# Layer norm of the rows behind attention: the scale and shift applied on ScalarE instead of VectorE

## The chip, the cores and the metric

The kernel runs on one core of a Trainium2 chip. The metric is the device time of one launch in microseconds (us). The names used below are those of the core's engines: TensorE (PE; its weight loads are PEld), VectorE (DVE), ScalarE (ACT), GpSimd (POOL) and SyncE (SP), each with its own queue of instructions that it works through in order.

## The reference

One transformer layer over 8 batches of 512 tokens of width 256: causal attention with 16 heads, a layer norm on the sum, a mixture of experts (16 experts, 6 for each token, and a shared one), and a second layer norm.

```
def _layernorm(x, axis=-1, eps=1e-05):
    m = jnp.mean(x, axis=axis, keepdims=True)
    v = jnp.var(x, axis=axis, keepdims=True)
    return (x - m) / jnp.sqrt(v + eps)
...
    x = L0_attn_x
    x = _layernorm(x + _L0_attn_ref(x, L0_attn_w_qkv, L0_attn_w_out), axis=-1)
    x = _layernorm(x + _L0_ffn_ref(x, ...), axis=-1)
    return x
```

The change touches the first of these two layer norms, for the rows of seven of the eight batches.

## The kernel before

**Stages.** The first part of the kernel (up to about 480 us of its span) is attention, batch by batch. Behind it come the shared expert (with the rest of the last batch in between), the blocks of routed experts, and the final sum with the second layer norm.

**The order inside a batch.** A batch `b` is four groups of four heads, `g` = 0 to 3, and each group has eight sub-steps `s` = 0 to 7. Each engine runs its own unrolled loop over `(g, s)`, and tables written by hand say what it does at which sub-step. On PE the string `PE_ORDER[g][s]` is the order of its work in a sub-step:

- `P`: `scores` (line 873), the key-by-query scores of this group that the softmax needs. There are twelve fills of a PSUM bank, numbered 0 to 11, and they take turns in two banks: fill n waits until ScalarE has done the exponential of fill n - 2 (`pe.wait_ge(exp_done, ...)`). Sub-step 0 has fills 0 and 1, sub-step 1 has 2 and 3, sub-step 2 has 4 and 5, sub-step 3 has 6 and 7, and 4 to 7 have one each. Fills 4 to 7 are 384 columns wide.
- `F` and `G`: `scores_for_max` (lines 854 and 860), scores of the group after the next, whose row maxima VectorE takes (`maxima`, line 1629); eleven fills in three banks, so that each waits for the maximum three before it.
- `A`: `attend` (line 885), probabilities times values of the group before, or the transposes of its result (line 911).
- `M`: one stage of the work in between, by the table `MISC`: projections for the next batch, the transpose of the maxima (`m`), and for the batch before it the output projection (`p0`, `p1`), the transposes of the normalised rows (`x0`, `x1`, line 917) and the router (`r`, `d`).

**ScalarE** (`iteration` under `@block.scalar`) does at each sub-step the first `PROBS_AHEAD[g][s]` of the exponentials (`probabilities`, line 1243), then what `MISC` gives it, then the rest of the exponentials. In group 2 this is: sub-step 1: exponentials 2 and 3, then two small copies for stage `m` (`shift_h` and `shift`, line 1234); sub-step 2: exponential 4, then 5; sub-step 3: 6 and 7, then `attn_T`; sub-step 4: 8, then the copies `t_hi` and `t_raw` of stage `x0`.

**VectorE** does at each sub-step its share of the maxima and a list of other work. The layer norm of batch `b - 1` runs in iteration `b`: the sum with the input into `x1p` at (1,4) and (1,6), the statistics `stats` and `mean_var` at (1,5) and (1,6); GpSimd makes `rstd` from them at (1,7) (`inverse_std`, lines 2127 and 2130); VectorE normalises two of the four row tiles of 128x256 at (2,1) and the other two at (2,2) (`normalize`, line 1645). The tables for group 2:

```
PE_ORDER[2] = ["FAPMG", "PFAMG", "FPMGA", "PAMFG", "FAMPG", "FPGAM", "AFPMG", "FPGAM"]
PROBS_AHEAD[2] = [1, 2, 1, 2, 1, 2, 1, 2]
MAXIMA_AHEAD[2] = [1, 2, 2, 1, 1, 2, 0, 2]
```

Stage `x0` stands at (2,4), ahead of `P` there; PE waits in it for both halves of the rows (`pe.wait_ge(x1_done, 2 * b)`). SyncE waits for the same count before it loads the next `x_res`. In the last of the seven iterations there are no maxima to take, and PE runs filler matmuls in their place (line 981). The rows of the eighth batch are normalised in the epilogue, by the old function on VectorE, which the change leaves there.

Of the kernel before, what the change touches and what calls it, by code (L numbers as in the profile page):

```python
# [24 lines left out]
P = 128  # L25
B, S, D = 8, 512, 256
# [3 lines left out]
QT = S // P  # L30
# [77 lines left out]
STATS_AT = {(1, 5): 0, (1, 6): 1}  # L108
INVERSE_AT = (1, 7)
NORMALIZE_AT = {(2, 1): 0, (2, 2): 1}  # L110
ROUTE_AT = {(3, 1): 0, (3, 2): 1, (3, 4): 2, (3, 5): 3, (3, 6): 4}
SOFTMAX_AT = (3, 2)

# [85 lines left out]
CLEARED, CONSTS = 11, 14  # L199
Y_PIECES = B - 1  # L200
Y_ROWS = P * -(-(T_ALL + P) // (P * Y_PIECES))
GAP, GAP2 = 352, 3672


def fills_of(g, s):

    done = sum(FILLS_OF_SUB[g][:s])
    return tuple(range(done, done + FILLS_OF_SUB[g][s]))
# [44 lines left out]
def postln_layer(nc, xT, x, wqk, wv, wo, gw, gb, ws, we, be, b13, b2s, out):  # L253
    fp32, f32r, bf16 = mybir.dt.float32, mybir.dt.float32r, mybir.dt.bfloat16
    i32, u32 = mybir.dt.int32, mybir.dt.uint32
    ALU, ACT, AX = mybir.AluOpType, mybir.ActivationFunctionType, mybir.AxisListType
# [5 lines left out]
    def sem(name):  # L262
        return ctx.enter_context(nc.semaphore(name))

    def sb(name, shape, dt=fp32, where=ctx):
        return where.enter_context(nc.sbuf_tensor(name, shape, dt))

    def sa(name, shape, dt=fp32):
        return sb(name, shape, dt, phase_a)

    with ctx:
# [12 lines left out]
        mean_var = sb("mean_var", [P, QT, 2])  # L284
        var_eps = sb("var_eps", [P, QT])
        rstd = sb("rstd", [P, QT])
        bias = sb("bias13", [P, 2, ST])
# [72 lines left out]
        expert_of = sa("expert_of", [P, 2])  # L360
        skipped_rows = sa("skipped_rows", [P, 2])
        table_rows = sa("table_rows", [4, P], i32)
        bias_rest = sa("bias_rest", [P, GAP2])
        x1p = [sa(f"x1p{n}", [P, QT, PAY]) for n in range(2)]
        index = [sa(f"index{n}", [P, QT * TOP_K], u32) for n in range(2)]
# [99 lines left out]
        t_lo_done = sem("t_lo_done")  # L465
        ln_step = sem("ln_step")
        rstd_step = sem("rstd_step")
        x1_done = sem("x1_done")
        x1_stored = sem("x1_stored")
        router_step = sem("router_step")  # L470
# [761 lines left out]
        def _(act):  # L1232
            def copy(dst, src, scale=1.0):
                return nc.scalar.activation(dst, src, ACT.Copy, scale=scale)  # L1234

            def probabilities(G, fills):
                for f in fills:
                    kt, heads = PROB_FILLS[f]
                    n, width = len(heads), S - kt * P
                    act.wait_ge(st_full, SF * G + (f + 1))  # L1240
                    if not (isinstance(G, int) and G == 0):
                        act.wait_ge(pv_done, 4 * G + (kt - 3))
                    nc.scalar.activation(probs[kt][:, heads[0]:heads[0] + n, :],  # L1243
                                         st[f % ST_BANKS][:, 0:n * width].rearrange("p (h t) -> p h t", h=n),
                                         ACT.Exp).then_inc(exp_done, 1)
# [21 lines left out]
            def transposed(misc, k):  # L1267

                copy(t_hi[:, k, :], misc)
                return copy(t_raw[:, k, :], misc)  # L1270

            def misc_stage(b, g, stage, no, misc=None):
# [34 lines left out]
                elif stage[0] == "x":  # L1307
                    k = int(stage[1])
                    act.wait_ge(t_lo_done, 4 * t + (k + 1))
                    transposed(misc, k).then_inc(misc_free[bank], 1)  # L1310

            def middle_part(nb, tile):
                act.wait_ge(rest_done, 4 * nb + (tile + 1))
                copy(parts[tile % 2][1][:, tile // 2, :], rest[:, tile % 2, :]).then_inc(part_m_done, 1)

            def read_attn(G):
                act.wait_ge(pv_done, 4 * G + 4)
                if not (isinstance(G, int) and G == 0):
                    act.wait_ge(recip_done, G)
                copy(attn_T[:], ov).then_inc(attn_T_done, 1)  # L1320
# [13 lines left out]
            def iteration(b, par):  # L1334
                whole = isinstance(b, int)
                for g in range(NG):
                    G = 4 * b + g
                    for s in range(SUBS):
                        probabilities(G, PROB_FILLS_OF_SUB[s][:PROBS_AHEAD[g][s]])
                        if s == READ_AT and not (whole and b == 0 and g == 0):  # L1340
                            read_attn(G - 1)
                        stage = MISC.get((g, s))
                        if stage and has(b, g, stage):
                            misc_stage(b, 1 - par if stage[0] == "v" else g, stage, fill_no(b, (g, s)))
                        if (g, s) in PARTS_AT and not (whole and b == LAST):
                            middle_part(b + 1, PARTS_AT[g, s])
                        if (g, s) == SOFTMAX_AT and not (whole and b == 0):
                            router_softmax(b - 1)
                        if (g, s) == SPLIT_X_AT and not (whole and b == LAST):
                            split_x(b + 2)  # L1350
                        if whole and b == LAST and (g, s) in FIRST_W_AT:
                            split_w(FIRST_W_AT[g, s])
                        if whole and b == LAST and (g, s) == SPLIT_FIRST_X1_AT:
                            split_x1(0)
                        probabilities(G, PROB_FILLS_OF_SUB[s][PROBS_AHEAD[g][s]:])
# [248 lines left out]
        def _(dve):  # L1604
# [38 lines left out]
            def normalize(buf, done, tiles=range(QT)):  # L1643
                for qt in tiles:
                    last = nc.vector.tensor_scalar(buf[:, qt, 0:D], buf[:, qt, 0:D], mean_var[:, qt, 0:1],
                                                   rstd[:, qt:qt + 1], ALU.subtract, ALU.mult)
                last.then_inc(done, 1)
# [173 lines left out]
            def iteration(b, par):  # L1821
                whole = isinstance(b, int)
                for g in range(NG):
                    G = 4 * b + g
                    for s in range(SUBS):
                        shifts = has(b, g, "m") and (g, s) in SHIFT_AT
                        first_group = whole and b == 0 and g == 0
                        maxima_fills = () if whole and 4 * b + g + 2 >= NG * B else fills_of(g, s)
                        if shifts:
                            split_shift(G + 1, (g + 1) % 2, fill_no(b, key_of("m", g)), 2 * SHIFT_AT[g, s])  # L1830
                        if s == NORM_AT and not first_group:
                            norm_rows(G - 1, (g - 1) % NG)
                        for f in maxima_fills[:MAXIMA_AHEAD[g][s]]:
                            maxima(G + 2, (g + 2) % NG, f, g % 2)
                        if shifts and SHIFT_AT[g, s] == 0:
                            split_shift(G + 1, (g + 1) % 2, fill_no(b, key_of("m", g)), 1)
                        if s == RECIP_AT and not first_group:
                            rows_recip(G - 1)
                        if (g, s) == RANK_AT and not (whole and b < 2):
                            rank(b - 2, par, fill_no(b - 1, key_of("d")))  # L1840
                        if not (whole and b == 0):
                            if (g, s) in SUM_AT:
                                stage = f"p{SUM_AT[g, s]}"
                                misc_stage(b, 1 - par, stage, fill_no(b, key_of(stage)))
                            if (g, s) in STATS_AT:
                                f = STATS_AT[g, s]
                                attn_stats(b, 1 - par, f, fill_no(b, key_of(f"p{f}")))
                            if (g, s) in NORMALIZE_AT:
                                f = NORMALIZE_AT[g, s]
                                dve.wait_ge(rstd_step, 2 * b)  # L1850
                                normalize(x1p[1 - par], x1_done, (2 * f, 2 * f + 1))
                            if (g, s) in ROUTE_AT:
                                route(b - 1, 1 - par, fill_no(b, key_of("r")), ROUTE_AT[g, s])
                        if whole and b == LAST and (g, s) in FIRST_W_AT:
                            split_w(FIRST_W_AT[g, s])
                        if whole and b == LAST and (g, s) == SPLIT_FIRST_X1_AT:
                            low_x1(0)
                        for f in maxima_fills[MAXIMA_AHEAD[g][s]:]:
                            maxima(G + 2, (g + 2) % NG, f, g % 2)
                        if (g, s) in REST_AT and not (whole and b == LAST):  # L1860
                            tile = REST_AT[g, s]
                            rest_of(b + 1, tile, fill_no(b, key_of(QK[tile])))
                        if (g, s) == LOW_X_AT and not (whole and b == LAST):
                            low_x_of(b + 2)
# [508 lines left out]
```

## Time and profile before

| | us |
|---|---|
| median of 3 runs (lowest, highest) | 1070.45 (1070.27, 1071.28) |
| the profiled execution | 1073.4 |
| its span (first to last instruction) | 1071.6 |
| PE busy | 993.2 (93%) |
| DVE busy | 811.9 (76%) |
| ACT busy | 734.7 (69%) |
| POOL busy | 752.0 (70%) |

The profile has a page with busy shares, and the trace behind it is asked for views: the chain of waits that ended last, a timeline of an engine in a window, the busy time of all engines in a window, the instructions of one source line. Times are microseconds from the start of the span. In a timeline a row is start, length, engine, line, operation, written tile and read tiles, and a count; a length over several instructions goes from the start of the first to the end of the last, and in square brackets stands the time that the engine had been idle and what ended it. A matmul's end is modelled, and neighbouring matmuls overlap.

### The profile page before, as it was taken

What the parts mean: (1) busy time and instruction counts of PE and PEld (TensorE: products, weight loads), DVE (VectorE), ACT (ScalarE), POOL (GpSimd) and SP (SyncE); (2) the same over time, 40 slices, a digit from 0 to 9 for tenths busy, and PEclk for the clock granted to TensorE, in tenths of its full rate; (3) what the DMA queues carried; (4) which work ended last, traced back from release to release, by engine and by line L of the source; (5) the groups of instructions that cost most, each with busy time, mean ns of one, the idle gap of its engine ahead of it and who ended that gap; (6) DMA issues with size and microseconds to landing.
All of it is one profiled execution on the core that took longest, in us unless ns stands there. A gap on an engine that the chain in (4) does not pass through costs nothing.

```text
span 1071.6 us, 27815 instructions
## 1 busy us (share of the span) xinstructions
PE 993.2 (93%) x7534; PEld 791.1 (74%) x7535; DVE 811.9 (76%) x2622; ACT 734.7 (69%) x1859; POOL 752.0 (70%) x677
## 2 busy tenths in 40 slices
PE   7899999999999998899899999999999999999982
PEld 4545555656565554459889999999999999999871
DVE  8776878888888888848767687777777777777496
ACT  4577566676666665667455598878888888888545
POOL 4224548888888888877754677777777777777576
PEclk8899999999999999999899999999999999999986
DMA  6633244555555555367778988878877878788793
GB/s 183 174 113 101 85 139 153 180 163 172 161 174 171 168 167 188 124 209 222 251 227 199 214 153 159 135 129 133 131 131 130 134 130 134 131 136 175 191 385 130
DMA packets 136716, 176.37 MB, mean 165 GB/s; under 512 B 19584, under 2 KB 113840, under 8 KB 136368
## 3 DMA queue, kind: packets, MB, share of 16 engines
q1 hardware_dynamic: 88016, 105.83, 33.4%
q0 software_dynamic: 39024, 54.29, 28.7%
q10 hardware_dynamic: 9584, 15.11, 4.7%
q8 instruction: 48, 0.79, 0.3%
q14 instruction: 44, 0.36, 0.1%
HBM read 73.68 MB, written 78.17 MB: 142 GB/s over the span
## 4 chain that ended last, share of the span: by engine, by line
PE 71%; DVE 16%; ACT 5%; issue 4%; DMA 1%; POOL 1%; SPq 1%; ACTq 0%; POOLq 0%; DVEq 0%
PE psum L1118 19%; PE psum L840 11%; PE psum L1145 7%; PE psum L885 5%; PE psum L1148 4%; PE psum L873 4%; DVE rowmax L1629 4%; PE psum L854 4%; PE psum L1101 4%; PE psum L1131 2%; ACT probs L1243 2%; PE psum L1132 2%; PE psum L1082 2%; PE psum L860 1%; PE psum L917 1%
## 5 line engine op out<-in xcount | busy, mean ns | idle before, releaser
L1243 ACT ACTIVATE probs<-psum 128x512 f32<-128x512 f32 (+2 forms) x384 | 186.5, 530 | 118.8 <-PE psum L873 116.7
L1629 DVE TENSOR_REDUCE rowmax<-psum 128x1 f32<-128x512 f32 (+3 forms) x352 | 212.1, 633 | 54.3 <-PE psum L860 52.0
L2188 POOL DMA_INDIRECT xs_d<-x1p,index x192 | 204.1, 1063 | 54.3 <-issue 39.4
L1118 PE MATMUL psum<-we_hi_lo,xb_hi 128*128 x828 | 206.7, 332 | 0.0
L1976 DVE TENSOR_TENSOR hb<-psum,hb 128x176 f32<-128x176 f32 x207 | 70.7, 342 | 96.7 <-ACT hb L1424 90.8
L2260 POOL DMA_INDIRECT x_d<-y_sb,tokens x69 | 108.5, 1572 | 49.5 <-issue 28.6
L2100 POOL TENSOR_SCALAR_AFFINE_SELECT probs<-probs 128x512 f32<-128x512 f32 x128 | 87.3, 682 | 78.6 <-ACT probs L1243 76.3
L1118 PEld LDWEIGHTS psum<-we_hi_lo,xb_hi 128*128 128x128 f32 x828 | 136.9, 188 | 2.9 <-issue 0.2
L854 PE MATMUL psum<-stack_k,stack_q 96*128 96x256 bf16 (+3 forms) x512 | 129.1, 310 | 7.6 <-DMA stack_k<-k_l 2.4
L2260 POOL DMA_INDIRECT z_d<-y_sb,tokens x69 | 108.6, 1573 | 38.2 <-issue 25.3
L1118 PE MATMUL psum<-we_hi_lo,xb_lo 128*128 x414 | 133.6, 323 | 0.0
L2260 POOL DMA_INDIRECT y_d<-y_sb,tokens x69 | 108.4, 1571 | 32.9 <-issue 25.3
L873 PE MATMUL psum<-stack_q,stack_k 99*128 99x256 bf16 (+3 forms) x512 | 116.8, 303 | 14.8 <-ACT probs L1243 12.4
L1443 ACT ACTIVATE y_sb<-psum,combine 128x256 f32<-128x256 f32 x207 | 99.0, 478 | 26.3 <-PE psum L1148 22.5
L1424 ACT ACTIVATE hb<-psum 128x176 f32<-128x176 f32 x207 | 65.9, 318 | 56.1 <-PE psum L1118 24.4
L885 PE MATMUL psum<-probs,values 128*32 128x512 f32 (+3 forms) x1024 | 92.8, 446 | 9.1 <-DVE attn L1706 8.1
L1145 PE MATMUL psum<-we_hi_lo,hb_hi 128*128 x414 | 101.0, 325 | 0.1
L873 PEld LDWEIGHTS psum<-stack_q,stack_k 99*128 99x128 bf16 x512 | 41.5, 98 | 71.5 <-ACT probs L1243 46.6
L1957 DVE TENSOR_TENSOR xb_lo<-psum,xb_hi 128x256 fp32r<-128x256 f32 x207 | 88.0, 425 | 7.3 <-ACT xb_hi L1234 0.9
L860 PE MATMUL psum<-causal,ident_bf 128*128 128x128 bf16 (+2 forms) x352 | 88.2, 251 | 0.0
L1234 ACT ACTIVATE psum<-bias_tab 128x352 f32 x183 | 85.3, 466 | 0.9 <-DVE hb L1976 0.9
L1148 PE MATMUL psum<-we_hi_lo,hb_hi 128*128 x414 | 83.0, 282 | 0.0
(227 smaller groups left out, 2553.9 us busy)
## 6 DMA issues: line engine op xcount, KB each, us to landing
xb<-xs_d SPq DMA_DIRECT2D x207, 138.0 KB
stack_q<-q_h SPq DMA_DIRECT2D x48, 128.0 KB
stack_k<-k_h SPq DMA_DIRECT2D x45, 128.0 KB
w_raw<-in_we SPq DMA_DIRECT2D x9, 608.0 KB, 4.4
xT_raw<-in_xT SPq DMA_DIRECT2D x9, 512.0 KB, 4.5
stack_q<-q_m SPq DMA_DIRECT2D x32, 128.0 KB
stack_k<-k_m SPq DMA_DIRECT2D x32, 128.0 KB
x_res<-in_x SPq DMA_DIRECT2D x8, 512.0 KB, 4.2
```

The source lines that it names most:

```text
L840: last = nc.tensor.matmul(dst, lhs(a, k), rhs(b, k), start=n == 0, stop=n == 3 * KD - 1)
L854: nc.tensor.matmul(sm[bank][:, i * width:(i + 1) * width], stack_q[par][0:STACK, head, qt * P:qt * P + P], stack_k[par][0:STACK, head, 0:w ...
L873: last = nc.tensor.matmul(st[f % ST_BANKS][:, i * width:(i + 1) * width], stack_k[par][0:STACK + SHIFT_ROWS, head, kt * P:kt * P + P], sta ...
L885: last = nc.tensor.matmul(ov[32 * j:32 * j + 32, kt * P:S], values[par][:, kt, GH * g + j, :], probs[kt][:, j, :], start=kt == 0, stop=kt ...
L1118: last = nc.tensor.matmul(uv, (xb_hi, xb_lo)[a][k % 2][:, d, :], w_flat[:, bass.ds(at + b * W_COLS + d * UP, UP)], start=False, stop=d == ...
L1145: nc.tensor.matmul(y, hb_lo[k % 2][:] if a else hb_hi[k % 2][:, 0, :], w_flat[:, bass.ds(at + b * W_COLS + W2_AT, D)], start=(a, b) == (0, ...
L1148: last = nc.tensor.matmul(y, packed, w_flat[:, bass.ds(at + b * W_COLS + W2_AT + D, D)], start=False, stop=b == 1)
L1243: nc.scalar.activation(probs[kt][:, heads[0]:heads[0] + n, :], st[f % ST_BANKS][:, 0:n * width].rearrange("p (h t) -> p h t", h=n), ACT.Ex ...
L1443: nc.scalar.activation(y_sb[k % 4][:], y_ps[k % 2][:, 0:D], ACT.Copy, scale=combine[:, k:k + 1]).then_inc(y_out, 1)
L1629: nc.vector.reduce_max(rowmax[gpar][:, heads[0]:heads[0] + n, qt], src, AX.X).then_inc(sm_free, 1)
L2188: nc.gpsimd.indirect_dma_start(out=xs_d[:, :], out_offset=bass.IndirectOffsetOnAxis(ap=index[tp][:, n:n + 1], axis=0), in_=x1p[tp][:, n // ...
L2260: nc.gpsimd.indirect_dma_start(out=(x1_d, z_d, y_d)[k % SUMS][:, :], out_offset=bass.IndirectOffsetOnAxis(ap=tokens[:, k:k + 1], axis=0), ...
```

## The change

VectorE no longer normalises the rows in iterations 1 to 7. It makes `ln_shift = -mean * rstd`, 128x4, in one instruction at (2,0), and ScalarE computes `rows * rstd + ln_shift` in place, four Identity activations of 128x256 in each of these iterations: two at (2,1), behind the two small copies of stage `m`, and two at (2,2), between exponentials 4 and 5. `x1_done` is raised by ScalarE, once at each place, as VectorE did.

```diff
 NORMALIZE_AT = {(2, 1): 0, (2, 2): 1}
+SHIFT_ROWS_AT = (2, 0)
...
-GAP, GAP2 = 352, 3672
+GAP, GAP2 = 352, 3664
...
+        ln_shift = sa("ln_shift", [P, QT])
...
+        ln_shift_done = sem("ln_shift_done")
...
+            def normalize(b, tp, f):
+                act.wait_ge(ln_shift_done, b)
+                for qt in (2 * f, 2 * f + 1):
+                    rows = x1p[tp][:, qt, 0:D]
+                    last = nc.scalar.activation(rows, rows, ACT.Identity, bias=ln_shift[:, qt:qt + 1], scale=rstd[:, qt:qt + 1])
+                last.then_inc(x1_done, 1)
...
                         if (g, s) in PARTS_AT and not (whole and b == LAST):
                             middle_part(b + 1, PARTS_AT[g, s])
+                        if (g, s) in NORMALIZE_AT and not (whole and b == 0):
+                            normalize(b, 1 - par, NORMALIZE_AT[g, s])
...
-                            if (g, s) in NORMALIZE_AT:
-                                f = NORMALIZE_AT[g, s]
+                            if (g, s) == SHIFT_ROWS_AT:
                                 dve.wait_ge(rstd_step, 2 * b)
-                                normalize(x1p[1 - par], x1_done, (2 * f, 2 * f + 1))
+                                nc.vector.scalar_tensor_tensor(ln_shift[:], mean_var[:, :, 0], -1.0, rstd[:], ALU.mult,
+                                                               ALU.mult).then_inc(ln_shift_done, 1)
```

## Rows read from the trace of the kernel before

**Rows 1.** The page, busy us, share of the span and instructions of each engine.
```profile
PE 993.2 (93%) x7534; PEld 791.1 (74%) x7535; DVE 811.9 (76%) x2622; ACT 734.7 (69%) x1859; POOL 752.0 (70%) x677
```

**Rows 2.** Busy time by window: one iteration; columns PE, PEld, DVE, ACT, POOL, granted clock, DMA.
```profile
188.00:244.00 56.00, 52.52 (x434) 31.78 (x433) 46.04 (x114) 37.65 (x85) 46.86 (x52) 1.00 0.55 168
```

**Rows 3.** The chain of waits that ended last, 174 to 179 us.
```profile
174.78 1.21 DVE x1p L1645 x2
...
177.38 0.66 DVE x1p L1645 x2
```

**Rows 4.** Who PE waited for, 132 to 188 us: total us, times, longest us.
```profile
PE psum L885 <- DVE attn L1706: 1.0, 1, 1.0
PE psum L917 <- DVE x1p L1645: 0.4, 1, 0.4
```

**Rows 5.** Timeline of ScalarE, iteration 2, from the small copies on.
```profile
175.26 0.25 ACT L1234 ACTIVATE shift<-psum 16x128 f32<-16x128 f32 x1
175.52 0.87 ACT L1243 ACTIVATE probs<-psum 128x384 f32<-128x384 f32 x2
...
179.06 0.60 ACT L1243 ACTIVATE probs<-psum 128x512 f32<-128x512 f32 x1 [0.95 <-PE psum L873]
...
180.51 0.62 ACT L1243 ACTIVATE probs<-psum 128x512 f32<-128x512 f32 x1
```

**Rows 6.** Timeline of TensorE in the same stretch.
```profile
176.37 0.50 PE L873 MATMUL psum<-stack_q,stack_k 99*128 99x384 bf16 x2
...
177.56 0.22 PE L860 MATMUL psum<-causal,ident_bf 128*128 128x128 bf16 x1
178.18 0.63 PE L917 MATMUL psum<-ident,x1p 128*128 128x128 f32 x4 [0.40 <-DVE x1p L1645]
...
181.18 0.28 PE L873 MATMUL psum<-stack_q,stack_k 99*128 99x128 bf16 x2
```

**Rows 7.** Line 1526, the second layer norm's Identity: durations (min/median/max ns), and a timeline row.
```profile
L1526 ACT ACTIVATE fin_x<-fin_x,fin_shift,fin_rstd x32: 583/586/602, 1034.0 to 1067.7; 128x256 f32<-128x256 f32 x32
...
1058.42 6.00 ACT L1526 ACTIVATE fin_x<-fin_x,fin_shift,fin_rstd 128x256 f32<-128x256 f32 x12 [3.70 <-DVE fin_shift L2034]
```

**Rows 8.** Timeline of TensorE in iteration 1, stage x0.
```profile
122.32 0.63 PE L917 MATMUL psum<-ident,x1p 128*128 128x128 f32 x4 [0.93 <-DVE x1p L1645]
```

**Rows 9.** Timelines of ScalarE and TensorE in iteration 7.
```profile
454.95 0.25 ACT L1234 ACTIVATE shift<-psum 16x128 f32<-16x128 f32 x1
455.37 0.87 ACT L1243 ACTIVATE probs<-psum 128x384 f32<-128x384 f32 x2 [0.17 <-PE psum L873]
...
456.22 0.50 PE L873 MATMUL psum<-stack_q,stack_k 99*128 99x384 bf16 x2
...
457.66 0.49 PE L917 MATMUL psum<-ident,x1p 128*128 128x128 f32 x3
```

**Rows 10.** Timeline of VectorE, iteration 2.
```profile
171.52 3.27 DVE L1629 TENSOR_REDUCE rowmax<-psum 128x2 f32<-128x512 f32 x5
174.70 1.29 DVE L1645 TENSOR_SCALAR x1p<-x1p,mean_var,rstd 128x256 f32<-128x256 f32 x2
...
177.96 0.75 DVE L1693 TENSOR_TENSOR shift_l<-shift_rest,shift_m 16x128 bf16<-16x128 f32 x1
```

**Rows 11.** Timeline of GpSimd, iteration 2.
```profile
172.15 1.05 POOL L2130 TENSOR_TENSOR rstd<-var_eps,half_neg 128x4 f32<-128x4 f32 x1
173.18 0.64 POOL L2100 TENSOR_SCALAR_AFFINE_SELECT probs<-probs 128x512 f32<-128x512 f32 x1
...
177.36 1.20 POOL L2188 DMA_INDIRECT xs_d<-x1p,index  x1 [0.30 <-issue]
```

**Rows 12.** Line 2034, the second layer norm's shift: durations in ns (min/median/max).
```profile
L2034 DVE SCALAR_TENSOR_TENSOR fin_shift<-fin_mv,fin_rstd x5: 128/924/1257, 1032.7 to 1066.1; 128x8 f32<-128x8 f32 x3, 128x4 f32<-128x4 f32 x2
```

**Rows 13.** Line 1396, where ScalarE turns from exponentials to Silu: its table loads.
```profile
L1396 ACT ACT_TABLE_LOAD  x2: 1283/1283/1283, 478.1 to 507.2; - x2
```

**Rows 14.** Busy time by window, shared expert's stretch; columns as in rows 2.
```profile
512.93:516.35 3.42, 3.42 (x16) 3.42 (x17) 1.80 (x10) 0.86 (x3) 2.51 (x4) 0.50 0.90 298
...
551.00:554.40 3.40, 3.40 (x31) 3.40 (x30) 2.55 (x6) 1.34 (x3) 2.49 (x4) 1.00 0.94 305
```

## The prediction

> **What bounds the kernel now.** I read the page first [rows 1]: PE is busy 93% of the span, VectorE 76%, ScalarE 69%. In the attention iterations it is the same picture at full clock: of 56 us PE is busy 52.5, VectorE 46.0, ScalarE 37.7 [rows 2]. PE is the bound, with some 3.5 us of holes in an iteration, and what counts is which engine makes or fills a hole. The chain of waits, read next, runs straight through the work that is moved: 1.21 us of it at (2,1) and 0.66 us at (2,2) [rows 3]. That looks like 1.9 us to be had in each iteration. The third view corrects this: PE's own waits charge to the normalisation only the 0.4 us before stage x0 [rows 4]. The chain counts VectorE's whole queue back from that short wait. So the most that a free VectorE can give here is about 0.5 us an iteration, and the question is what ScalarE's queue does to the same place. That needs the timelines of ScalarE and PE side by side [rows 5, 6].
>
> **Removed from VectorE.** Four TENSOR_SCALAR in each of seven iterations: from 174.70 to the next maxima and again before 177.96 [rows 10], 1.21 and 0.66 us of its queue [rows 3]. The maxima behind them come earlier. PE waits for few of them: behind the last score fill of sub-step 4 (its last matmul starts at 177.56, 0.06 us of work at this rate) x0 could start at 177.62 and starts at 178.18 [rows 6]. Gain if nothing else changes: 0.56 us.
>
> **Added to VectorE.** One scalar_tensor_tensor of 128x4 at (2,0). The same operation at the end of the kernel took 0.13 to 1.26 us [rows 12]; no row shows it at this place. Its slot is behind three of the five maxima that start at 171.52, so near 173.3, and rstd is written at 173.20 [rows 10, 11]: no real wait. If GpSimd's mask holds it until 173.82 [rows 11] it costs 0.5 us, at the long end 1.26 us. VectorE would then be done with its maxima at 175.2 (at 176.0 at the long end), where its next work needs ScalarE's small copies, done at 175.51 [rows 5], and PE asks for the maximum behind them only for the fill of 177.4. I cost it at nothing; its cover is the 1.21 us that VectorE has just been relieved of. The shift_l part that the next group's DMA waits for comes earlier, too. SyncE's x_res load waits for x1_done, which comes within 0.2 us of where it did. No DMA is added.
>
> **Added to ScalarE.** Four Identity activations in place on 128x256, with scale and bias from SBUF. The second layer norm has this very instruction: 586 ns each, and twelve back to back took 6.00 us, so one occupies (6.00 - 0.586) / 11 = 0.49 us of the queue [rows 7]. Low bound from the nearest cheaper rows: two 384-column exponentials take 0.87 us [rows 5], and with a single one at 0.49 us the spacing is 0.38; less for 128 columns fewer, some 0.3. I take 0.49, since form, operands and memory are the same, and keep 0.3. Four are 1.97 us, and the place decides what they do. They stand ahead of exponential 4 (two) and of exponential 5 (two). Behind exponential 5, PE waits with scores 7, because the score fills take turns in two banks; and behind scores 7 in PE's queue stand attend, two fills for the maxima, and x0.
>
> Step by step in iteration 2:
> - Exponentials 4 and 5 now run from 175.52 and end at 176.39; the copies leave the queue at 175.42, 0.10 us sooner [rows 5]. Exponential 5 will end at 176.39 - 0.10 + 1.97 = 178.26.
> - PE starts 0.06 us after an exponential that it waits for (180.51 + 0.62 = 181.13, and PE at 181.18) [rows 5, 6]: scores 7 at 178.32. It starts now at 176.37 + 0.17 = 176.54, without waiting (two matmuls of 384 columns take 0.50 us, one 0.33) [rows 6].
> - From scores 7 to the point where x0 could start are 177.62 - 176.54 = 1.08 us of PE's work. x0 starts at 178.32 + 1.08 = 179.40; both halves of the rows are ready by 177.9.
> - Now it starts at 178.18. Loss: 1.22 us. In a formula: 4 x (queue time of one) - 0.75 us, so the change breaks even at 0.19 us for one Identity.
>
> **Does the delay stay?** Behind x0 the chain is scores 8, exponential 8, the copies t_hi and t_raw, exponential 9 and PE again at 181.18; none of it had room, and ScalarE's 0.95 us of idle time before 179.06 is only the wait for scores 8 [rows 5, 6]. Then PE runs without a hole into the router matmuls, and VectorE waits for these. I find no later wait for something that is not itself shifted, so the loss is taken whole.
>
> **First and last.** In iteration 1 x0 waited 0.93 us for VectorE, not 0.40 [rows 8], with the same steps before: the loss is 1.22 - 0.53 = 0.69. In iteration 7 PE doesn't wait at x0. Exponentials 4 and 5 end at 455.37 + 0.87 = 456.24; the copies leave the queue at 455.11, so 5 ends at 456.24 - 0.26 + 1.97 = 457.95, scores 7 start at 458.01 against 456.39, and x0 follows both times 1.27 us later [rows 9]: loss 1.62.
>
> **Sum.** 0.69 + 5 x 1.22 + 1.62 = 8.4 us. The profiled execution took 1073.4 us, its span 1071.6, some 3 us over the median of the runs, 0.3%; the loss lies inside the span and doesn't scale with that. So 1081.8 for a profiled execution and 1070.45 + 8.4 = 1078.9 us for the median, 0.8% slower. With 0.3 us for one Identity the middle iterations lose 0.45, the first nothing and the last 0.85: 3.1 us, 1073.5.
>
> **The clock.** All attention iterations ran at granted clock 1.00 [rows 2]. The new hole before scores 7 is about 1 us, with some 0.5 us before scores 6; the longest wait there now is 1.0 [rows 4]. I expect the clock to hold. In the shared expert's stretch it fell to 0.50 for 3.4 us after PE had waited, and 16 matmuls ran where 31 ran at 1.00 [rows 14]: about 1.6 us for each such fall. All of this stretch comes 8 us later and its falls need not recur alike; one or two more or fewer make 3 us either way, which I put into the range.
>
> **Rivals.**
> - *A, faster: VectorE was the wait, and ScalarE's idle time takes the new work.* For it: the chain runs through the normalisation [rows 3], and ScalarE idles 0.95 us before 179.06 [rows 5]. Against it: that idle time is behind exponentials 4 to 7, not in front. It decides if an Identity takes under 0.19 us of the queue. Then x0 starts up to 0.56 us earlier in five iterations, 1.1 in the first, nothing in the last: 3.9 us, 1066.5 us. 8%.
> - *B, no change: the delay is made good later*, by the earlier maxima and the freer GpSimd. For it: PE has 3.5 us of holes in an iteration [rows 2]. Against it: the holes that I find follow work that shifts along. 1070.5 us. 8%.
> - *C, ScalarE reloads its tables* at each turn between Exp and Identity. A load took 1.28 us [rows 13]; four turns in an iteration, seven iterations, are 36 us on top: 1115 us. For it: no row shows Identity next to Exp. Against it: the copies of line 1234 stand between exponentials with no load, and line 1526 follows Silu with none. 3%. The Trainium skill (ScalarE: Activation LUTs, "Table sets: the hidden batching unit") says that cheap functions such as copy and identity are in every set, so that no load is needed; the same page ("What ACT_TABLE_LOAD costs") gives about 2.66 us for a switch with its drain, by which this rival would cost 74 us. The trace agrees for copy, and has 1.28 us for the load itself.
> - *D, slower by more*: the new hole pulls the clock down in the attention stage. One fall of 3.4 us an iteration at 1.6 us each adds 11 us: 1090 us. 4%.
> - *The forecast*, loss at exponentials 4 and 5: 77%.
>
> **Range and chances.** 1072.5 to 1082.5: from the loss with the short Identity less some of the clock's 3 us, to the forecast plus those 3 us. That leaves out A, most of B, C and D. Within 0.2% (2.1 us, what measurements of this kernel can tell from none) lie B and a little of the forecast: 9%. Faster 8%, slower 83%.
>
> **What would show it.** Right: line 1645 gone from VectorE in iterations 1 to 7; four Identity rows of 0.58 us each; PE waiting for ScalarE at scores 7 by about 1 us; no wait at x0 for the rows; an iteration 57.1 us long instead of 55.9. Wrong: exponential 5 ending before 177.2 in such an iteration, or the iteration as long as before although scores 7 waits.

## The result, and the profile after

The changed kernel takes 1082.3 us (median of 4 runs, 1081.74 to 1083.26), the kernel before beside it 1070.87: ratio 1.0117, 95% interval 1.0102 to 1.0132. The two medians stand 11.4 us apart; by the ratio, which is used from here on, the change costs about 12.5 us (0.0117 x 1071; 10.9 to 14.1 by the interval). The sign was forecast, the size was not: 8.4 us had been forecast, and a time of at most 1082.5. The median of the four runs lies just under that; by the ratio, applied to the 1070.45 us from which the forecast started, the time is 1083.0, above it.

The page of the changed kernel, busy us by engine: VectorE has lost 11.4 us, ScalarE has gained 13.2, PE is where it was, and the span is 8.3 us longer.

```profile
PE 994.6 (92%) x7534; PEld 792.6 (73%) x7535; DVE 800.5 (74%) x2601; ACT 747.9 (69%) x1887; POOL 749.5 (69%) x677
```

ScalarE in iteration 2 of the changed kernel (timeline, as in rows 5; line 1319 is the new activation, 1246 the exponentials, 1237 the copies):

```profile
174.97 0.25 ACT L1237 ACTIVATE shift<-psum 16x128 f32<-16x128 f32 x1
175.12 1.07 ACT L1319 ACTIVATE x1p<-x1p,ln_shift,rstd 128x256 f32<-128x256 f32 x2
176.10 0.46 ACT L1246 ACTIVATE probs<-psum 128x384 f32<-128x384 f32 x1
176.47 1.07 ACT L1319 ACTIVATE x1p<-x1p,ln_shift,rstd 128x256 f32<-128x256 f32 x2
177.46 1.38 ACT L1246 ACTIVATE probs<-psum 128x384 f32<-128x384 f32 x3
178.73 0.60 ACT L1237 ACTIVATE attn_T<-psum 128x512 f32<-128x512 f32 x1
179.91 0.60 ACT L1246 ACTIVATE probs<-psum 128x512 f32<-128x512 f32 x1 [0.58 <-PE psum L876]
```

TensorE in the same stretch (timeline, as in rows 6; line 876 is scores, 888 attend, 920 the transposes of x0):

```profile
176.62 0.34 PE L876 MATMUL psum<-stack_q,stack_k 99*128 99x384 bf16 x1 [0.47 <-ACT probs L1246]
177.97 0.34 PE L876 MATMUL psum<-stack_q,stack_k 99*128 99x384 bf16 x1 [1.02 <-ACT probs L1246]
178.24 0.43 PE L888 MATMUL psum<-probs,values 128*32 128x128 f32 x8
...
179.00 0.22 PE L863 MATMUL psum<-causal,ident_bf 128*128 128x128 bf16 x1
179.06 0.60 PE L920 MATMUL psum<-ident,x1p 128*128 128x128 f32 x4
```

The reader should follow one chain through both. The exponentials 4 and 5 stood back to back from 175.52 [rows 5]; now each has a pair of Identities ahead of it. Scores 6 waits 0.47 us for exponential 4, scores 7 waits 1.02 us for exponential 5, and x0 follows 1.09 us behind scores 7 with no wait of its own, where it had waited 0.40 us for VectorE [rows 6]. PE's waits in the window of rows 4, the kernel before first, then the changed one:

```profile
PE psum L873 <- ACT probs L1243: 1.5, 4, 0.7
```

```profile
PE psum L876 <- ACT probs L1246: 3.0, 6, 1.0
PE psum L888 <- DVE attn L1718: 1.0, 1, 1.0
```

The line of x0 is gone, and the wait for exponentials has six places with 3.0 us where the kernel before had four with 1.5. The next view shows what I had not reckoned with, busy time by window with the granted clock in the third column from the right:

```profile
235.50:238.90 3.40, 3.40 (x23) 2.23 (x23) 1.02 (x3) 1.60 (x4) 1.61 (x2) 0.50 0.44 110
351.50:354.90 3.40, 3.40 (x18) 2.59 (x17) 1.58 (x3) 1.95 (x5) 1.60 (x2) 0.50 0.63 171
409.60:413.00 3.40, 3.40 (x23) 2.23 (x16) 1.28 (x3) 1.72 (x4) 1.61 (x2) 0.50 0.55 158
178.00:181.40 3.40, 3.40 (x35) 2.73 (x36) 2.28 (x5) 2.76 (x7) 1.60 (x2) 1.00 0.37 120
```

In iterations 3, 5 and 6 the clock fell to 0.50, the lower of its two levels (1.2 GHz), 0.5 to 1.5 us before x0, that is 0.2 to 0.8 us behind the end of the second new hole; PE then ran some 18 to 23 matmuls in a stretch in which it ran 35 at full clock in iteration 2. In iterations 1, 2, 4 and 7 the same two holes stand (0.3 to 0.5 us and 1.0 us), and the clock held. Rows 2 show one iteration of the kernel before; a longer window of it has no fall from 66 us on, through all of iterations 1 to 7:

```profile
66.00:512.00 446.00, 414.48 (x3417) 255.83 (x3409) 354.90 (x877) 297.07 (x649) 331.89 (x361) 1.00 0.51 159
```

Its falls in attention lie before that, in the first batch (the last one from 52.1 to 55.5 us).

Where the time sits, by the start of x0: from iteration 1 to iteration 7 there are 468.69 - 122.07 = 346.6 us, against 457.66 - 122.32 = 335.3 before [rows 8, 9], 11.3 more. From x0 of iteration 7 to the end of the span there are 611.2 us against 613.9: in the shared expert's stretch the profiled execution of the kernel before had three falls of the clock, this one a single one. So the spans differ by 8.3 us, just what had been forecast, but by luck: three falls added 3.3 us in attention, and behind it two falls fewer go with 2.7 us less. The timed runs differ by more.

### The profile page after: what moved, and what is told of

It is laid out like the page before. It is cut to its first block, busy times and chain, and to the rows that moved or that the text cites. A ratio compares the mean times of both kernels' runs of the same rounds, so it can differ in the third digit from the quotient of the medians.

```text
span 1079.9 us, 27822 instructions
## 1 busy us (share of the span) xinstructions
PE 994.6 (92%) x7534; PEld 792.6 (73%) x7535; DVE 800.5 (74%) x2601; ACT 747.9 (69%) x1887; POOL 749.5 (69%) x677
## 4 chain that ended last, share of the span: by engine, by line
PE 74%; DVE 11%; ACT 6%; issue 5%; POOL 2%; DMA 0%; SPq 0%; ACTq 0%; POOLq 0%; DVEq 0%
PE psum L1121 19%; PE psum L843 12%; PE psum L1148 7%; PE psum L888 6%; PE psum L876 5%; PE psum L857 5%; PE psum L1151 4%; PE psum L1104 4%; DVE rowmax L1641 3%; ACT probs L1246 3%; PE psum L1134 2%; PE psum L1135 2%; PE psum L1085 2%; PE psum L863 2%; PE psum L920 1%
## 5 line engine op out<-in xcount | busy, mean ns | idle before, releaser
L876 PE MATMUL psum<-stack_q,stack_k 99*128 99x256 bf16 (+3 forms) x512 | 119.2, 306 | 24.5 <-ACT probs L1246 22.7
L1148 PE MATMUL psum<-we_hi_lo,hb_hi 128*128 x414 | 101.0, 326 | 0.1
L857 PEld LDWEIGHTS psum<-stack_k,stack_q 96*128 96x128 bf16 x512 | 45.3, 100 | 52.8 <-issue 25.4
```

The source lines that it names most:

```text
L857: nc.tensor.matmul(sm[bank][:, i * width:(i + 1) * width], stack_q[par][0:STACK, head, qt * P:qt * P + P], stack_k[par][0:STACK, head, 0:w ...
L876: last = nc.tensor.matmul(st[f % ST_BANKS][:, i * width:(i + 1) * width], stack_k[par][0:STACK + SHIFT_ROWS, head, kt * P:kt * P + P], sta ...
L1148: nc.tensor.matmul(y, hb_lo[k % 2][:] if a else hb_hi[k % 2][:, 0, :], w_flat[:, bass.ds(at + b * W_COLS + W2_AT, D)], start=(a, b) == (0, ...
```

## The experiments

Eight kernels ran, e1 to e4 on one chip and e5 to e8 on another; each ratio is to the kernel before on the same chip, with its 95% interval.

| | what it is | ratio | interval |
|---|---|---|---|
| e1_nobody | nobody normalises in iterations 1 to 7 (leaves out scale and shift of the rows) | 0.9957 | 0.9941 to 0.9973 |
| e2_both | VectorE as before, four Identities on ScalarE on top | 1.0119 | 1.0097 to 1.0140 |
| e3_filled | changed, new holes filled with matmuls | 1.0069 | 1.0051 to 1.0087 |
| e4_early | changed, Identities at other places on ScalarE | 0.9956 | 0.9942 to 0.9970 |
| e5_pe_order | changed, attend and a fill ahead of scores 6 | 1.0023 | 1.0014 to 1.0033 |
| e6_half | changed, second pair of rows on VectorE | 1.0008 | 0.9999 to 1.0016 |
| e7_immediates | changed, copies instead of Identities (leaves out scale and shift too) | 1.0024 | 1.0011 to 1.0036 |
| e8_changed | changed, once more | 1.0118 | 1.0103 to 1.0133 |

### What VectorE's relief is worth: e1_nobody

```diff
             def normalize(b, tp, f):
                 act.wait_ge(ln_shift_done, b)
-                for qt in (2 * f, 2 * f + 1):
-                    rows = x1p[tp][:, qt, 0:D]
-                    last = nc.scalar.activation(rows, rows, ACT.Identity, bias=ln_shift[:, qt:qt + 1], scale=rstd[:, qt:qt + 1])
-                last.then_inc(x1_done, 1)
+                act.sem_inc(x1_done, 1)
```

> The changed kernel without its 28 Identity activations: ScalarE only raises the count at the two places, so the rows of seven batches go on unnormalised (left out: the layer norm's scale and shift there). Theory (the loss is ScalarE's new work ahead of exponentials 4 and 5; VectorE's relief is worth little): x0 starts 0.56 us earlier than in the kernel before in five iterations, 1.1 us in the first, not at all in the last, 3.9 us in sum, ratio 0.996 to 0.998; no wait of TensorE at scores 6 and 7; no fall of the clock in the attention stage. Rival (VectorE was the bound, as the chain of waits suggests): 1.9 us an iteration, 13 us, ratio 0.988.

0.9957, so 4.6 us faster (2.9 to 6.3). x0 waits no more, and most iterations take 55.3 us against 55.9:

```profile
174.53 0.49 PE L920 MATMUL psum<-ident,x1p 128*128 128x128 f32 x3
```

The ratio is by a hair under the range of the expectation and far from 0.988: of the 1.9 us that the chain charged to line 1645 [rows 3] some 0.5 to 0.6 us an iteration were to be had.

### What ScalarE's work costs by itself: e2_both

```diff
+        twin = sa("twin", [P, QT, D])
...
+            def twin_of(b, f):
+                act.wait_ge(rstd_step, 2 * b)
+                for n in range(2):
+                    nc.scalar.activation(twin[:, 2 * f + n, :], pad_block[:, 0:D], ACT.Identity,
+                                         bias=half_neg[:, n:n + 1], scale=half_neg[:, n + 2:n + 3])
...
+                        if (g, s) in NORMALIZE_AT and not (whole and b == 0):
+                            twin_of(b, NORMALIZE_AT[g, s])
```

> The kernel before, VectorE normalising as it did, plus the same four Identity activations an iteration on ScalarE at the same places, from a constant tile into a spare one. Theory: TensorE waits 0.5 us before scores 6 and 1.0 us before scores 7 as in the changed kernel, x0 then finds its rows ready, and the whole loss is there: ratio 1.010 to 1.013. Rival (the loss has to do with the rows' way over ScalarE, the shift made on VectorE, or its new wait): without that the ratio stays under 1.004.

1.0119, the same as the change, with VectorE's work in place. TensorE's timeline in iteration 2 (here line 874 is scores and 918 is x0):

```profile
175.82 0.34 PE L874 MATMUL psum<-stack_q,stack_k 99*128 99x384 bf16 x1 [0.47 <-ACT probs L1244]
177.18 0.34 PE L874 MATMUL psum<-stack_q,stack_k 99*128 99x384 bf16 x1 [1.02 <-ACT probs L1244]
...
178.26 0.60 PE L918 MATMUL psum<-ident,x1p 128*128 128x128 f32 x4
```

The same two holes, to the hundredth. Even the clock's falls are there, in the same three iterations. The loss belongs to the work on ScalarE at this place; the new shift on VectorE and the rows' way have no part in it that the intervals (some 2 us wide to each side) could tell. VectorE's relief, some 0.5 us, is worth nothing behind these holes: here, with VectorE's old work still in place, x0 finds its rows ready without it.

### Is it the clock, too: e3_filled and e8_changed

In `scores`, ahead of its wait; the bank is the one that x0 overwrites next:

```diff
-            def scores(G, par, g, s):
+            def scores(G, par, g, s, b=0):
...
                     n = SF * G + f
+                    if g == 2 and f in (6, 7) and b > 0:
+                        warm_up((2, 4)[f - 6], fill(fill_no(b, (2, 4)))[0])
                     if not (isinstance(n, int) and n < ST_BANKS):
                         pe.wait_ge(exp_done, n - (ST_BANKS - 1))
```

> The changed kernel with filler matmuls of 512 columns in its two new holes on TensorE, two before scores 6 and four before scores 7 in iterations 1 to 7, into the bank that x0 takes next. Theory (some 4 of the 12 us are three falls of the clock to 0.50 at 235.5, 351.5 and 409.6 us of the span, which begin at these holes): no fall in the attention stage, the holes as long as before, ratio 1.007 to 1.009. Rival (the falls cost nothing, or come from elsewhere): ratio 1.011 to 1.013 as for the changed kernel, or more, if the fillers delay scores 6 and 7 themselves.

> The changed kernel once more, beside the others. Theory: ratio 1.010 to 1.013, iterations of 57.0 us where the clock holds, and two to four falls of the clock to 0.50 in the attention stage. Rival (the falls are an accident of one execution): none here, iterations all 57.0 us, with the same time.

With fillers 1.0069, without them 1.0118. TensorE's timeline with fillers (line 986) in iteration 2, and below it the granted clock of this kernel over the attention stage:

```profile
177.09 0.61 PE L986 MATMUL psum<-ones_bf 128*128 128x512 bf16 x2
177.63 0.34 PE L878 MATMUL psum<-stack_q,stack_k 99*128 99x384 bf16 x1
177.80 1.03 PE L986 MATMUL psum<-ones_bf 128*128 128x512 bf16 x4
178.98 0.34 PE L878 MATMUL psum<-stack_q,stack_k 99*128 99x384 bf16 x1
```

```profile
66.00:480.00 414.00, 387.46 (x3138) 225.79 (x3130) 314.26 (x753) 284.04 (x629) 300.30 (x330) 1.00 0.48 148
```

Scores 7 starts 1.35 us behind scores 6 as in the changed kernel, so nothing that the holes wait for has moved; but there is no fall. The unfilled kernel, run again in e8, has the three falls in the same iterations as in its first profile (at 234.5, 350.5 and 408.6 us), and so has e2_both: they are no accident of one execution. One of them in e8:

```profile
234.50:237.90 3.40, 3.40 (x23) 2.23 (x23) 1.03 (x3) 1.60 (x4) 1.61 (x2) 0.50 0.49 112
```

From x0 of iteration 1 to x0 of iteration 7 there are 343.3 us with fillers and 346.6 and 346.7 without: three falls, 1.1 us each. By the ratios the fillers are worth 0.0118 - 0.0069 = 0.49%, 5.2 us; the intervals leave 3.3 us open as well. On one and the same chip e2_both, which has the same holes unfilled, and e3 can be compared directly: medians of 1083.73 and 1079.19 us, 4.5 us apart.

The timed runs have a mean granted clock each, and it bears this out. It is 0.9735 on average in e2's four runs, 0.9788 in e3's six and 0.9793 in the nineteen of the kernel before beside them. A fall of 3.4 us to half clock takes 1.7 us of full clock, so by an estimate e2's runs have (0.9793 - 0.9735) x 1080 / 1.7 = 3.7 falls more than the kernel before, and e3's 0.3. The difference of 3.4 falls goes with 4.5 us, 1.3 us each: about as many falls as the profiles show, at a slightly higher price.

### The law of the loss: e6_half, e7_immediates, e5_pe_order

e6 leaves the second pair to VectorE at (2,2):

```diff
-                        if (g, s) in NORMALIZE_AT and not (whole and b == 0):
-                            normalize(b, 1 - par, NORMALIZE_AT[g, s])
+                        if (g, s) == (2, 1) and not (whole and b == 0):
+                            normalize(b, 1 - par, 0)
...
+                            if (g, s) == (2, 2):
+                                normalize(x1p[1 - par], x1_done, (2, 3))
```

> The changed kernel with only the first pair of rows on ScalarE (before exponential 4); the second pair stays on VectorE at (2,2). Theory (loss of a middle iteration = number of Identities x 0.49 us - 0.75 us): 0.2 us a middle iteration, gain of 0.3 in the first, loss of 0.6 in the last, 1.5 us in sum, no falls of the clock, ratio 1.000 to 1.003. Rival (the second pair is what costs nothing, or the cost is a fixed one of handing over to ScalarE): half the loss or more, ratio over 1.005.

1.0008, 0.9 us, with an interval that takes in no loss at all. An iteration takes 56.0 us, and scores 6 and 7 start as a pair behind one wait:

```profile
176.25 0.71 PE L876 MATMUL psum<-stack_q,stack_k 99*128 99x384 bf16 x2 [0.47 <-ACT probs L1246]
```

e7 has four instructions as the changed kernel, but shorter ones:

```diff
-                    last = nc.scalar.activation(rows, rows, ACT.Identity, bias=ln_shift[:, qt:qt + 1], scale=rstd[:, qt:qt + 1])
+                    last = nc.scalar.activation(rows, rows, ACT.Copy, scale=1.0)
```

> The changed kernel with its 28 Identity activations replaced by copies in place with a scale of 1.0 given in the instruction, instead of scale and bias read from SBUF; this leaves out the layer norm's scale and shift in seven batches. Theory (loss = 4 x queue time of one - 0.75 us): a copy of 128x256 within SBUF took 0.41 us at line 1234, so some 0.31 us of the queue; 0.5 us a middle iteration, 3.3 us in sum, no or fewer falls of the clock, ratio 1.002 to 1.005. Rival (the hole comes from the number of instructions and waits, not from their length): ratio 1.010 or more.

1.0024, 2.6 us, and four of the six stretches from one x0 to the next take 56.25 to 56.36 us where the changed kernel at full clock has 57.0. The durations of the two (line 1319, ns, the changed kernel above, e7 below):

```profile
L1319 ACT ACTIVATE x1p<-x1p,ln_shift,rstd x28: 583/583/586, 118.1 to 466.4; 128x256 f32<-128x256 f32 x28
```

```profile
L1319 ACT ACTIVATE x1p<-x1p x28: 398/398/400, 118.2 to 457.9; 128x256 f32<-128x256 f32 x28
```

Four times the 0.185 us between them are 0.74 us, and the iteration is 0.7 us shorter. So the loss goes with the time that stands ahead of exponential 5. Neither of the two has a fall of the clock in iterations 1 to 7.

e5 turns the order on TensorE at (2,3):

```diff
-    ["FAPMG", "PFAMG", "FPMGA", "PAMFG", "FAMPG", "FPGAM", "AFPMG", "FPGAM"],
+    ["FAPMG", "PFAMG", "FPMGA", "AFPMG", "FAMPG", "FPGAM", "AFPMG", "FPGAM"],
```

> The changed kernel with PE_ORDER[2][3] turned from PAMFG to AFPMG: attend and the fill for the maxima (0.6 us of work) go ahead of scores 6 and 7, into the hole that ScalarE makes. Theory (the loss is a hole in TensorE's queue before scores 7, with work behind it that need not wait): x0 comes 0.6 us earlier than in the changed kernel, so an iteration of about 56.4 us instead of 57.0, 3 to 4 us of loss without falls of the clock, ratio 1.003 to 1.006. Rival (ScalarE's queue sets the pace by itself, whatever TensorE does meanwhile): ratio over 1.009.

1.0023, just under the range of the expectation. The hole before scores 6 is gone and the one before scores 7 is still 1.02 us long, but x0 follows it by 0.40 us now and not by 1.09:

```profile
176.44 0.34 PE L876 MATMUL psum<-stack_q,stack_k 99*128 99x384 bf16 x1 [1.02 <-ACT probs L1246]
...
176.84 0.60 PE L920 MATMUL psum<-ident,x1p 128*128 128x128 f32 x4
```

Three of the six stretches from x0 to x0 take 56.3 to 56.4 us, and only one fall of the clock is left in the stage, in iteration 7 at 454.8 us, some 5 us ahead of x0, so not at the new hole. With 0.6 us of work moved in front, the change's loss sinks from 12.5 to 2.5 us. Some 4 to 5 us of that are the hole's filling (0.6 to 0.7 us in seven iterations); the other 5 to 6 are, roughly, what the clock had cost by e3. That split is argued, not measured.

### Another place on ScalarE: e4_early

```diff
+                        if (g, s) == (2, 1) and not (whole and b == 0):
+                            normalize(b, 1 - par, 0)
                         stage = MISC.get((g, s))
...
-                        if (g, s) in NORMALIZE_AT and not (whole and b == 0):
-                            normalize(b, 1 - par, NORMALIZE_AT[g, s])
...
                         probabilities(G, PROB_FILLS_OF_SUB[s][PROBS_AHEAD[g][s]:])
+                        if (g, s) == (2, 2) and not (whole and b == 0):
+                            normalize(b, 1 - par, 1)
```

> The changed kernel with ScalarE's first pair of Identities ahead of the two small copies of stage m, where ScalarE had 0.67 us of idle time, and the second pair behind exponential 5 instead of before it. Theory: scores 7 waits for nothing new, x0 starts about 0.4 us earlier than in the kernel before (177.7 instead of 178.2 us in iteration 2), ratio 0.995 to 0.999. Rival (ScalarE's queue is too full wherever the work is put): ratio over 1.003.

0.9956, 4.7 us faster than the kernel before and as fast as e1, which does no such work at all. In the kernel before, ScalarE stood idle for 0.67 us in front of the small copies, and e4 puts the first pair there. ScalarE's timeline in iteration 2, a row of the kernel before and then e4:

```profile
175.08 0.27 ACT L1234 ACTIVATE shift_h<-psum 16x128 bf16<-16x128 f32 x1 [0.67 <-PE psum L905]
```

```profile
169.52 1.67 ACT L1246 ACTIVATE probs<-psum 128x512 f32<-128x512 f32 x3
171.09 1.08 ACT L1319 ACTIVATE x1p<-x1p,ln_shift,rstd 128x256 f32<-128x256 f32 x2
172.07 0.25 ACT L1237 ACTIVATE shift_h<-psum 16x128 bf16<-16x128 f32 x1
172.22 0.25 ACT L1237 ACTIVATE shift<-psum 16x128 f32<-16x128 f32 x1
172.38 0.83 ACT L1246 ACTIVATE probs<-psum 128x384 f32<-128x384 f32 x2
173.12 1.08 ACT L1319 ACTIVATE x1p<-x1p,ln_shift,rstd 128x256 f32<-128x256 f32 x2
174.10 0.83 ACT L1246 ACTIVATE probs<-psum 128x384 f32<-128x384 f32 x2
```

Exponentials 4 and 5 come at once behind the copies, and the second pair stands behind the two exponentials. x0 starts at 174.40 without a wait. The same four instructions cost 12.5 us at one place and at another nothing that can be told from e1 (the intervals leave some 2 us). In the queue the places lie close together: the first pair has moved past two small copies, the second past one exponential.

## Why the prediction was wrong

- **What bounds the kernel**: right. PE's own waits, not the chain, gave the size of what VectorE could give back: 0.56 us an iteration forecast, 0.5 to 0.6 measured (e1).
- **Removed from and added to VectorE**: right. The shift took 0.54 us at its place, inside the bounds of 0.13 and 1.26, and VectorE then idled 0.5 us for ScalarE's copies, as its cover had said. The prediction's case of GpSimd's mask holding it for 0.5 us is what came: in each of the seven iterations the shift began while the mask (line 2112) ran and ended 0.01 to 0.02 us behind it. In iteration 2, VectorE and GpSimd:

```profile
173.00 0.55 DVE L1862 SCALAR_TENSOR_TENSOR ln_shift<-mean_var,rstd 128x4 f32<-128x4 f32 x1
```

```profile
172.89 0.64 POOL L2112 TENSOR_SCALAR_AFFINE_SELECT probs<-probs 128x512 f32<-128x512 f32 x1
```

- **Four Identities at 0.49 us of the queue ahead of exponential 5**: right. They took 583 ns each, and the two pairs kept 1.97 us of the queue; with half of them (e6) or with shorter ones (e7) the loss shrank as the formula says.
- **Scores 7 waits, x0 1.08 us behind it; 1.22 us an iteration**: right. From the copy `shift_h` to x0 there are 3.10 us before and 4.27 after in iteration 2, 1.17 more; in the first iteration 0.63 more (0.69 forecast) and in the last 1.58 more (1.62 forecast). That makes 0.63 + 5 x 1.17 + 1.58 = 8.1 us with the clock at full. An iteration at full clock took 57.0 us; 57.1 had been forecast. (PE's start behind an exponential was put at 0.06 us where the rows give 181.18 - 181.13 = 0.05; nothing hangs on it.)
- **The delay stays**: right; with the clock held by fillers (e3) the loss is 0.69%, 7.4 us (5.5 to 9.3), against 8.4 forecast.
- **"I expect the clock to hold"**: this is the step that failed. It put the clock's cost in the attention stage at nothing. Its reason was that the new 1.0 us hole is no longer than the longest wait of the trace before, also 1.0 us. For one such hole that holds: e5 has the 1.02 us hole alone in iterations 1 to 6, and no fall there. But it named the hole of 0.5 us before scores 6 without asking what the two do together. With both, three of seven iterations fell to the lower clock, 1.1 us each in the profile (1.6 had been taken for a fall), 4.5 to 5.2 us in the timed runs. Rival D named the mechanism, but with a fall in every iteration and a chance of 4%. The range held three microseconds for the clock, and for the shared expert's stretch only; the falls in attention alone used up more than that. (Forecast plus 3 us is 1081.9; the range's 1082.5 has no working for the rest.)
- Rivals A, B and C: A had its largest gain nearly to the point (3.9 us forecast for a free ScalarE, 4.6 in e1 and 4.7 in e4), but its condition, Identities under 0.19 us, wasn't met. B fell with e3, where 7.4 us of loss stay with the clock held. C fell with the timelines: exponentials and Identities alternate with no table load between them.

What stays open: the profile's three falls account for 3.3 us, the timed runs for 4.5 to 5.2 us, with 3.3 inside the interval. Why the clock fell in iterations 3, 5 and 6 and not in the other four, which have the same holes, no run shows. Nor is it known which smaller pair of holes is safe: e6 has only the one of 0.47 us, e7 has 0.10 and 0.65, e5 only the one of 1.02 us, and none of them has a fall at this place.

## What to carry to other kernels

Here, moving work to the engine with the lower busy share helped only at a place in its queue behind which nobody waits: find the instruction that the bounding engine waits for next, and put the new work behind it or into the idle time in front of it. A short wait of the bounding engine that the chain explains with a long stretch of another's work was worth the wait here (0.5 us), not the stretch (1.9 us). And when a change makes new holes in TensorE's work, cost the clock as well as the holes; an independent piece of its own work moved into a hole can pay twice, as in e5.

## What was not expected of the hardware

Behind two waits of 0.47 and 1.02 us, whose ends lie 1.35 us apart, TensorE's clock fell to 1.2 GHz in three of seven iterations, although PE was busy for 53.3 of 58 us around the first of them (188 to 246 us of the span); in all three executions profiled with these holes the falls came in the same iterations. With six filler matmuls in them the clock held.
